# Four recurrent layers on one core: the maxima of the last attention moved among the last layer's expert pairs

## What is computed

```python
x = L0_attn_x
xn = _layernorm(x, axis=-1)
...
# layer 2: linear attention, 16 experts, 4 chosen by softmax of gates
s = _L2_attn_ref(xn, L2_attn_W_qkv, L2_attn_W_out, L2_attn_b_out)
g = _silu(_L2_ffn_ref(xn, L2_ffn_gate_w, ...))
x = x + s * g
# layer 3: softmax attention with 16 heads of 8, 64 experts, 8 chosen in groups
q, k, v = ...                                  # 16 heads, 512 x 8 each, per batch
weights = softmax(einsum('bhtk,bhsk->bhts', q, k) * scale)
out = einsum('bhts,bhsk->bhtk', weights, v)
norms = jnp.linalg.norm(out, axis=-1)
denom = jnp.maximum(norms.mean(axis=(0, 2)), 1e-05)    # over all batches
proj = (einsum('bhtk,hkd->bhtd', out / denom, Wo) + bo) * gate
s = proj.sum(axis=1) / H
g = _silu(y + shared)       # y: 64 experts of width 64, each silu(x Wg) * (x Wu) * gate, times Wd
x = x + s * g
```

## Time and profile before

| | |
|---|---|
| median of 3 runs | 3910.12 us (3902.26 to 3915.28) |
| the profiled execution | 3902.76 us |
| its span in the trace | 3901.0 us |
| PE busy | 3082.5 us, 79% of the span |
| DVE, ACT, POOL busy | 62%, 43%, 15% |
| granted TensorE clock, mean | 0.877 of full |
| HBM | 302.74 MB read, 49.66 MB written |

### The profile page before, as it was taken

How to read it: one execution, slowest core, us unless ns; L and a number is a source line. 1 busy time by engine, 2 the same in 40 slices (tenths; PEclk the granted TensorE clock), 3 DMA queues, 4 the chain that set the end, 5 groups by cost and what they waited for, 6 DMA issues and landing times.

```text
span 3901.0 us, 43769 instructions
## 1 busy us (share of the span) xinstructions
PE 3082.5 (79%) x16082; PEld 1568.3 (40%) x16174; DVE 2433.6 (62%) x4576; ACT 1661.2 (43%) x2458; POOL 598.0 (15%) x425
## 2 busy tenths in 40 slices
PE   3557868997699867998499867998689976996588
PEld 1124423553245433553245432554235532464145
DVE  4634875568656775568755776568755785533442
ACT  3404615464254624465154633456154642532231
POOL 2001101311023010321013010321013110211030
PEclk8568879998799979998799979998799988997796
DMA  3241274302842164402842046412743138412261
GB/s 111 30 90 57 47 136 122 110 23 80 134 138 67 38 100 132 138 21 62 153 128 86 20 106 116 154 33 52 133 130 101 32 84 131 134 57 62 59 198 46
DMA packets 332807, 355.92 MB, mean 91 GB/s; under 512 B 99425, under 2 KB 265121, under 8 KB 330977
## 3 DMA queue, kind: packets, MB, share of 16 engines
q1 hardware_dynamic: 332593, 353.12, 38.6%
HBM read 302.74 MB, written 49.66 MB: 90 GB/s over the span
## 4 chain that ended last, share of the span: by engine, by line
PE 52%; DVE 22%; DMA 7%; ACT 6%; issue 4%; SPq 4%; POOL 3%; another core or an unknown queue 2%; ACTq 0%; DVEq 0%; POOLq 0%
PE PS L1799 6%; PE PS L1822 5%; PE PS L1826 5%; PE PS L1653 5%; PE PS L1661 5%; DMA U<-band_scratch 4%; PE PS L1097 3%; DVE U L885 3%; PE PS L1767 3%; SPq L671 3%; DVE U L892 3%; PE PS L1778 3%; DVE MX L1590 2%; POOL D L1398 2%
## 5 line engine op out<-in xcount | busy, mean ns | idle before, releaser
L1398 POOL TENSOR_TENSOR D<-D,GW 128x512 f32<-128x512 f32 x320 | 436.0, 1364 | 1443.1 <-ACT D L1471 1205.4
L777 ACT ACTIVATE U<-U 128x2048 f32<-128x2048 f32 x256 | 487.9, 1909 | 180.1 <-DVE U L885 97.1
L1639 DVE SCALAR_TENSOR_TENSOR D<-D,PS 128x512 f32<-128x512 f32 x336 | 228.7, 681 | 408.4 <-ACT D L1475 287.5
L1471 ACT ACTIVATE D<-PS 128x512 f32<-128x512 f32 x336 | 200.1, 595 | 596.7 <-PE PS L1822 596.7
L1799 PEld LDWEIGHTS PS<-WST,D 128*128 128x128 f32 (+1 forms) x2688 | 353.4, 198 | 174.6 <-DVE D L1644 103.4
L1799 PE MATMUL PS<-WST,D 128*128 128x128 f32 (+1 forms) x2688 | 380.2, 286 | 30.2 <-DVE D L1644 30.0
L1826 PE MATMUL PS<-XT,WST 128*128 128x512 f32 (+1 forms) x672 | 371.9, 636 | 31.9 <-DVE D L1639 30.8
L892 DVE SCALAR_TENSOR_TENSOR U<-PP,RD,QB 128x512 f32<-128x512 f32 x512 | 361.9, 773 | 45.4 <-ACT QB L774 26.7
L1097 PE MATMUL PS<-U,resident 128*32 128x512 f32 x2048 | 305.1, 676 | 104.1 <-ACT U L777 104.1
L1822 PE MATMUL PS<-XT,WST 128*128 128x512 f32 (+1 forms) x672 | 367.0, 629 | 9.7 <-DMA WST<-in_pairs_dram 6.4
L1590 DVE TENSOR_REDUCE MX<-PS 128x2 f32<-128x1024 f32 x256 | 297.0, 1219 | 122.6 <-PE PS L1745 122.4
(11 more groups left out here) (345 smaller groups left out, 3878.3 us busy)
## 6 DMA issues: line engine op xcount, KB each, us to landing
GW<-gates_scratch SPq DMA_DIRECT2D x320, 256.0 KB, 4.4
WST<-in_pairs_dram SPq DMA_DIRECT2D x336, 192.0 KB, 2.4
U<-band_scratch SPq DMA_DIRECT2D x32, 1280.0 KB, 15.3
UU<-in_w_dram SPq DMA_DIRECT2D x64, 512.0 KB, 7.4
UU<-pad_scratch SPq DMA_DIRECT2D x8, 1792.0 KB
UU<-q_scratch SPq DMA_DIRECT2D x24, 384.0 KB
UU<-k_scratch SPq DMA_DIRECT2D x24, 384.0 KB
e_scratch<-D SPq DMA_DIRECT2D x8, 1024.0 KB, 4.7
```

The costliest lines, as they stand in the source:

```text
L777: e.activation(ring(i), ring(i), ACT.Gelu).then_inc(S["act"], 1)
L1398: e.tensor_tensor(AV[:, n % 3, :], AV[:, n % 3, :], GW[:, p // 2 % GWS, p % 2, :], ALU.mult).then_inc(S["gated"], 1)
```

## The change

- A third thread C (`c_pe`, `c_dve`, `c_act`, `c_sp`) takes layer 3's split, stacks, S1, maxima and their transposition. S1 uses one bank, `PZ(2)`: 64 products, each of which waits for the maximum of the one before, and 64 maxima of one bank.
- The 33 pairs of layer 3 come first, as soon as the gates are there, with C's steps among them. S2, the values and the sums' selection follow behind the pairs. The two products that spread the sums over rows are steps of S2 (the two `None` in `B_STEPS`), ACT copies them to `RC`, now in the gates' tiles (`G4`), and reciprocals read them there.
- The sum of norms (`norm_sum`, `norm_copy`, `norm_store`) is made within FFN1 of the next batch, for the last batch at the end.
- W1's first four experts are loaded into `GW` when the last gates are used, the other four into `UU` when S2 is done. FFN1 waits for the last exponential, its first `down` into `PZ(3)` for the norms.
- In layer 2 the gates' scores come ahead of q, k, v, and the gates ahead of the attention's last product. The gates' rows go through `XN` rather than `LO`.
- The loads for the end come behind the pairs of the last batch.
- All due times are new; B's steps begin earlier against A's.

```diff
-TURN = 426.70
+TURN = 425.50
...
-        w1slot = lambda x: UU[:, 2 * FF * ((x + 4) % 8):2 * FF * ((x + 4) % 8) + 2 * FF].rearrange("p (k f) -> p k f", k=2)
+        w1slot = lambda x: (GWF, UU)[x // 4][:, 2 * FF * (x % 4):2 * FF * (x % 4) + 2 * FF].rearrange("p (k f) -> p k f", k=2)
...
+            e.wait_ge(S["gate_act"], at("gate_act", b, 4))
+            e.dma_start(gw_dram, LO(b)[0:E3, :, :].rearrange("p j c -> p (j c)")).then_inc(S["gw_out"], 16)
+            yield
+            e.wait_ge(S["gw_out"], at("gw_out", b, 32))
+            for q in range(GWS):
+                gate_load(e, b, 3, q)
+            for p in range(PAIRS3):
+                yield
+                if PAIRS2 + WS + p < PAIRS:
+                    pair_load(e, b, PAIRS2 + WS + p)
+                if p % 2 == 1 and GWS + p // 2 < E3 // 4:
+                    yield
+                    gate_load(e, b, 3, GWS + p // 2)
...
+        B_STEPS = list(range(0, 42)) + [None] + list(range(42, 64)) + [None]
...
-            for k in range(32):
-                yield
-                hd, j = k // 2, 2 * (k % 2)
+        def c_dve(e, b):
...
+            for k in range(64):
+                yield
                 e.wait_ge(S["s1_3"], at("s1_3", b, k + 1))
-                e.tensor_reduce(MX3[:, j:j + 2, hd], PSall[:, 4 + j:6 + j, :], AX.X, ALU.max).then_inc(S["max3"], 1)
+                e.tensor_reduce(MX3[:, k % NT:k % NT + 1, k // NT], PSall[:, 6:7, :], AX.X, ALU.max).then_inc(S["max3"], 1)
...
+        def c_pe(e, b):
+            for k in range(64):
+                yield
+                hd, j = k // NT, k % NT
+                if k == 0:
+                    e.wait_ge(S["stacked3"], at("stacked3", b, 96))
+                    e.wait_ge(S["padded3"], at("padded3", b, 16))
+                    e.wait_ge(S["qk3"], at("qk3", b, 2))
+                else:
+                    e.wait_ge(S["max3"], at("max3", b, k))
+                e.matmul(PZ(2), QS3[:, hd, P * j:P * j + P], KS3[:, hd, :], start=True, stop=True).then_inc(S["s1_3"], 1)
...
-            weave(thread(a_pe, e, 0), thread(b_pe, e, 1))
+            weave(thread(a_pe, e, 0), thread(b_pe, e, 1), thread(c_pe, e, 1))
```

More of the change, by code:

```diff
@@ L1429, in b_act @@
             e.wait_ge(S["b_f"], at("b_f", b, 2))
+            e.wait_ge(S["gw_out"], at("gw_out", b, 16))
             e.activation(XN(b), GB(b), ACT.Tanh).then_inc(S["b_t"], 1)
-            yield from b_norm_act(e, b, 3, 151)
+            yield from b_norm_act(e, b, 3, 141)
+            yield
+            e.wait_ge(S["gate_ps"], at("gate_ps", b, 3))
+            e.activation(SCO[:, :, :], PZ(0)[:, 0:NT * E3].rearrange("p (j n) -> p j n", j=NT), ACT.Tanh, scale=0.5).then_inc(S["gate_act"], 1)
             for k in range(2):
@@ L1695, in b_pe @@
             w2 = cn("qkv2")
+            for j in range(NT):
+                last = e.matmul(PZ(0)[:, 2 * P + E2 * j:2 * P + E2 * j + E2], XT(b)[:, P * j:P * j + P], cn("gates")[:, 8:8 + E2], start=(j == 0), stop=False, skip_group_check=True)
+            last.then_inc(S["gate_ps"], 1)
             e.matmul(PZ(1), w2[:, 0:C], XT(b), start=True, stop=True).then_inc(S["l2_ps"], 1)
@@ L1699, in b_pe @@
             last.then_inc(S["l2_ps"], 1)
-            for j in range(NT):
-                e.matmul(PZ(0)[:, 2 * P + E2 * j:2 * P + E2 * j + E2], XT(b)[:, P * j:P * j + P], cn("gates")[:, 8:8 + E2], start=(j == 0), stop=False, skip_group_check=True)
             yield
+            e.wait_ge(S["gate_dve"], at("gate_dve", b, 1))
             e.wait_ge(S["l2_dve"], at("l2_dve", b, 1))
@@ L1711, in b_pe @@
             yield
+            e.wait_ge(S["gate_dve"], at("gate_dve", b, 3))
+            for j in range(NT):
+                last = e.transpose(PZ(0)[0:E2, P * j:P * j + P], GT[:, j, 0:E2], ident)
+            last.then_inc(S["gate_ps"], 1)
+            yield
             e.wait_ge(S["l2_dve"], at("l2_dve", b, 4))
@@ L1715, in b_pe @@
             last.then_inc(S["l2_ps"], 1)
-            yield
-            e.wait_ge(S["gate_dve"], at("gate_dve", b, 3))
-            for j in range(NT):
-                last = e.transpose(PZ(2)[0:E2, P * j:P * j + P], GT[:, j, 0:E2], ident)
-            last.then_inc(S["gate_ps"], 1)
             yield from b_pe_pairs(e, b, 2)
@@ L1725, in b_pe @@
             w3 = cn("wqkv3")
+            for j in range(NT):
+                last = e.matmul(PZ(0)[:, E3 * j:E3 * j + E3], XT(b)[:, P * j:P * j + P], cn("gates")[:, 24:88], start=(j == 0), stop=(j == NT - 1), skip_group_check=True)
+            last.then_inc(S["gate_ps"], 1)
             for k in range(2):
@@ L1752, in b_pe @@
             last.then_inc(S["gate_ps"], 1)
-            yield
-            e.wait_ge(S["nm3"], at("nm3", b, 1))
-            for j in range(NT):
-                last = e.transpose(PZB(1)[0:48, P * j:P * j + P], NM3[:, j, :], identb[:, :])
-            last.then_inc(S["nm_t3"], 1)
+            yield from b_pe_pairs(e, b, 3)
             def weighted(s):
@@ L1785, in b_pe, with norm_sum @@
             yield
-            e.wait_ge(S["os3"], at("os3", b, 2))
-            e.matmul(PZ(2), cn("sel_den"), OS3[:, 0, :], start=True, stop=True).then_inc(S["den3"], 1)
-            yield from b_pe_pairs(e, b, 3)
+            if b == B - 1:
+                norm_sum(e, b)
+        def norm_sum(e, b):
+            e.wait_ge(S["nrm3"], at("nrm3", b, 4))
+            for h in range(2):
+                last = e.matmul(PZ(3)[32 * h:32 * h + 8, :], cn("sum_group"), RC[:, h, :], start=True, stop=True)
+            last.then_inc(S["den3"], 1)
+        def c_pe(e, b):
+            for k in range(64):
+                yield
+                hd, j = k // NT, k % NT
+                if k == 0:
+                    e.wait_ge(S["stacked3"], at("stacked3", b, 96))
+                    e.wait_ge(S["padded3"], at("padded3", b, 16))
+                    e.wait_ge(S["qk3"], at("qk3", b, 2))
+                else:
+                    e.wait_ge(S["max3"], at("max3", b, k))
+                e.matmul(PZ(2), QS3[:, hd, P * j:P * j + P], KS3[:, hd, :], start=True, stop=True).then_inc(S["s1_3"], 1)
+            yield
+            e.wait_ge(S["nm3"], at("nm3", b, 1))
+            for j in range(NT):
+                last = e.transpose(PZB(2)[0:48, P * j:P * j + P], NM3[:, j, :], identb[:, :])
+            last.then_inc(S["nm_t3"], 1)
         def b_pe_pairs(e, b, l):
@@ L1795, in down @@
                 e.wait_ge(S["av"], at("av", b, n + 1))
-                if l == 2 and p == 0:
-                    e.wait_ge(S["l2_dve"], at("l2_dve", b, 5))
+                if p == 0:
+                    if l == 2:
+                        e.wait_ge(S["l2_dve"], at("l2_dve", b, 5))
+                    else:
+                        e.wait_ge(S["v3"], at("v3", b, 1))
                 for j in range(NT):
@@ L1854, in sp_before_final @@
                 e.wait_ge(S[s], at(s, B - 1, 0))
-            for k in range(B - 1):
+            for k in range(B - 2):
                 final_load(e, k, "fin_in")
```

319 lines of the change are left out of this document (167 added, 152 removed), and 180 rows, old and new, of tables (PER, STARTS).

## The result

| | before | with the change |
|---|---|---|
| median | 3906.68 us (4 runs) | 3976.77 us (4 runs, 3963.84 to 3980.57) |
| ratio, 95% interval | | 1.0171 (1.0140 to 1.0202) |
| span of the profiled execution | 3901.0 us | 3977.6 us |
| one full turn (mean of the seven, from one point of FFN1 to the same point) | 446.7 us | 460.2 us |

The change costs 1.7%. The forecast was 3876 us and faster; the range, up to 3940, doesn't hold it. A second measurement (e15) gave 1.0176.

A forecast was written before the change was run, and what follows sets the result against it. PE was taken as the bound: 370.8 us busy of a 447.4 us turn, plus 76.6 waiting. Seven turns +14, start -15.5, last turn -33 make -34.5 on 3901.0, so 3866.5, or 3876 on the median's scale; range 3800 to 3940.

The forecast's parts named there:

- The start, -15.5: Before the first full turn: FFN1 of batch 0 begins near 333.1 instead of 348.60, -15.5 us, bounds 0 and -15.5.
- Gates' chain, 14: Full turn after layer 3's v: PE idles 14 us while DVE makes the gates and they are spread over rows.
- Stacks, `e` and skew, 13: Full turn: gates' transfers queue behind stacks, `e` and its skewed load on SP, costing PE 13 us more idle time.
- the first product on POOL, 4: Full turn, among layer 3's pairs: the first product on POOL and its sums cost PE 4 us of idle time.
- Weights behind the bands, 11.5 + 10: Full turn: PE waits 11.5 us for pair weights behind the bands' stores, bounds 0 and 18, and 10 for bands' loads.
- The first rival: Full turn: pair weights starve behind bands' stores, PE waiting some 20 us; turn +10.5, 3935 us, slower; chance 0.23.
- The sum of the turn: Full turn: idle 52.5 us against 45.6, +7, less 5 for layer 2, rest unchanged: +2, giving 449.4.
- layer 2's -5: Layer 2: with gates first, 5 of 8.3 us of PE's waits at the gates' products and first `down` go.
- The last turn, -33: Last turn, B alone: 198 us against 225.7, -28, and layer 2's 5, together -33; bounds -20 and -42.
- No wait for L1664 above a microsecond: Sign to check in the last turn: among the pairs, no wait for L1664 should exceed a microsecond.
- the weights starve: Full turn: bands' stores hold up pair weights on SP's queue; decides from +6.9 a turn; chance 0.23.
- items 2 and 4: Full turn's idle list: gates behind stacks, `e` and skewed load (13 us); weights behind bands' stores and loads (11.5 + 10).

The follow-up runs named there:

- e15: The changed kernel again, nothing altered, run on the same chip as several follow-ups: 3980.84 us, 1.0176 to the kernel before.
- e1: The changed kernel with the bands' stores cut to 2 of 16 heads from the second batch on: 3885.62 us, 0.9937 to the kernel before.
- e3: The changed kernel with layer 3's weights from pair 5 on issued by ACT instead of SP: 3998.37 us, 1.0229 to the kernel before.
- e12: The changed kernel with FFN1 products that need nothing of A put first, and the sum of norms right at FFN1's start: 3938.51 us, 1.0067.
- e14: e12 with the bands' stores also cut to 2 of 16 heads as in e1: 3843.11 us, 0.9819 to the kernel before.
- e6: The changed kernel with bands' stores 3 and 4 behind weights of pairs 5 to 8, weights of pairs 9 to 12 among stores and bands' loads: 3973.84 us, 1.0163.
- e5: The changed kernel with bands' stores 3 and 4 moved on SP behind the weights of pairs 5 to 8: 3989.60 us, 1.0199.
- e7: The changed kernel with A's L932 ahead of B's gates on DVE and the store of `e` ahead of the stacks' loads on SP: 3984.37 us, 1.0186.
- e9: The changed kernel with the stacks' loads behind `e`'s store, skewed load and first gates on SP, and S1 later: 4147.17 us, 1.0531.
- e2: The kernel before with its bands' stores cut to 2 of 16 heads from the second batch on: 3894.30 us, 0.9960.
- e4: The changed kernel with all steps of threads B and C due 10 us later against A's: 4308.50 us, 1.1017.

## Why the prediction was wrong

**The start, -15.5: half right, on a misread row.** It came to -8.4. I took the row at 348.60 for FFN1's first product; it is the first of its second expert. The first stood at 341.81:

```profile
341.81 1.88 PE L1653 MATMUL PS<-XT,UU 128*128 128x512 f32 x4
```

With the change it stands at 317.90, ahead of the end of A. But behind the four products up of the first expert PE waits for A's reciprocal and for `mix`, so that FFN1 goes on at 340.17, not near 333.

**Gates' chain, 14: right.** 13.58.

**Stacks, `e` and skew, 13, and the first product on POOL, 4: right in kind, both too dear.** 7.2 at L1150 and 1.1 at the first product down, 8.3 together; `e` landed in 12.6.

**Weights behind the bands, 11.5 + 10: right in kind, the size near.** The weights behind L684 landed in 11.6 us. PE waits 12.7 for the pair behind the stores, and 0.8 later, 13.5; 10 for the bands' loads was too much. e1 shows that 13.9 us a turn go with the stores. The first rival, which wanted 20 there, had the sign and not the size; its 20 us of waiting were never reached. As for queue order, in e3 the weights land no sooner on another ring, so SP's order alone is not the cause.

**The sum of the turn: wrong, and this is the step that failed.** My idle time "from v to the point where A's bands are used up" was 52.5 for 45.6. From v's end to the end of A's projection it is 44.4 (122.62 less 78.18):

```profile
1905.90:2028.52 122.62, 78.18 (x415) 44.26 (x415) 74.91 (x178) 26.23 (x44) 21.55 (x17) 0.82 0.92 178
```

That is less than I said, and no more than before: 8 us too dear, which by luck hides part of the rest. The failure lies outside of it: I gave the rest of the turn nothing ("the rest of the turn keeps its work"), and that was false. Pairs, which wait for nothing of A, had stood beside A's last chain; I moved them away with the change and did not ask what they had covered. At FFN1's start PE now waits 5.2 + 4.7 + 4.0 for 3.2, 10.7 more. And it waits 6.9 for 1.0 at L1118 (L1105 before), where A's layer 0 ends: 16.6 us together.

A second part of the error is layer 2's -5, a saving of the last turn that I carried into the full turns. There was nothing to save there: in a full turn of before PE doesn't wait at L1719 and waits 2.1 at the first product down, and with the change it waits 1.2, 1.5 and 2.0 at L1771, L1780 and L1877.

Less waiting in A's layer 0 gives back 6 (3.6 for 9.7). So the sum should have read -1 for the stretch, +16.6, -6 and nothing for layer 2: some +9 or +10, with 13.5 measured. The remaining 3 to 4 I can't place; in the trace of before the missing records show as idle time, and smaller waits of the norms and of layer 2 go both ways.

What was tested of this is FFN1's start: 3938.51 us (e12) for 3980.84 (e15) on one chip, 42 of the 69 that the change costs there. The 5.9 at L1118 is read from the waits, and no run fills it. The stores and this hole are separate costs: taking both away (e14) gives 0.9819. That is a kernel with band stores left out, so it shows what the holes cost and not what can be had.

**The clock: not in the sum.** I took durations at whatever clock the rows had. Where two traces of the same PE work are complete, they differ by 24 us of PE's busy time: 3073.1 at a clock of 0.881 in e1, 3097.1 at 0.868 with the change. In e6 both kinds of turns stand in one kernel, 7 us apart. What of the change's own loss the clock makes the traces don't show.

**The last turn, -33: one term mis-sized.** The first product down came 39.8 us behind layer 3's first product (41 forecast; the gates' scores now stand there, 1.8 us ahead of q and k); S2 took 45.5 (46); the tail 13.7 (14); layer 2 gave 5.1 (5). But the 33 pairs with S1 among them took 116.4 us, from 3725.49 to 3841.9, where I took 97 with bounds of 92 and 110. PE's row in that turn, and a window of the pairs, which shows PE as the bound:

```profile
3706.21 1.03 PE L1799 MATMUL PS<-consts,G 128*64 128x128 f32 x4 [14.41 <-DVE G L1629]
...
3717.41 0.39 PE L1858 MATMUL PS<-UU 128*128 128x512 bf16 x1 [4.07 <-DMA UU<-k_scratch]
```

```profile
3730.00:3845.00 115.00, 102.66 (x447) 57.29 (x445) 80.47 (x127) 35.71 (x67) 38.29 (x30) 0.99 0.47 145
```

Gates and stacks hold the first pair as forecast. The pairs' time was there to be counted: a pair and two products of S1 take 3.14 us in the trace (1974.27 to 1977.41), 33 of them 103.6, and PE waited 10.2 for maxima on top. I had let S1's 64 products vanish into pairs that were already at PE's limit. From layer 3's first product to the norms' load it took 216.3 us for 225.7: of the 28 us that I gave to this stretch, 9.4 came. FFN1's last run took 5.6 more (53.1 for 47.4, from the first product up of its second expert to the last product up), with the norms of the batch before in it. "No wait for L1664 above a microsecond" held among the pairs but for one of 1.15; there were seventeen of them.

The rivals: "the weights starve" had the right side at 0.23, and the point from which it decides (+6.9 a turn) was passed at 13.5; but not by its mechanism alone. e1 takes 13.9 a turn away, and FFN1's start, which the rival doesn't name, costs 6 a turn beside it (42 us over seven, e12). The range ended at +10 a turn, a bound made from the transfers alone. Its lower bound of -8 doesn't follow from the list: without items 2 and 4 the 52.5 are 18, which is 28 less than 45.6. And the factor 1.0019 leaves out the 1.8 us between span and execution; 3876 is 3866.5 and the whole 9.2.

## What to carry to other kernels

When dense work is moved to cover a hole, price the place that it leaves with the same care as the place that it goes to: list who ran beside it there, and whose chain is bare afterwards. In a stretch in which the DMA engines are full, reordering the change's transfers only chose who waits (e3, e5, e6, e7, e9); taking the bands' stores out paid (e1, 13.9 us a turn). An order is worth another trial once another hole is filled: that of e6 gained nothing clear on the change and 0.0057 on e12. An engine that is busy without a gap has no room for "hidden" products: count them at full price.

## What the runs showed that I had not expected

- The same four stores of 256 KB cost 2.1 us a turn where stacks and bands stand beside them (e2) and 13.9 where weights for PE do (e1).
- Moving the weights to ACT's issue (e3) left PE's wait for them as it was, 97.5 us for 92.1, and beside the bands' transfers they took 9.1 to 12.6 us to reach PE on either queue.
- One kernel runs turns of 453.5 and of 460.3 us (e6), with PE's busy time 370.6 and 377.3 and a granted clock of 0.91 and 0.89. The order of e6 gave 0.0008 to 0.0013 on the change and 0.0057 on e12, where the clock of the turns shown is 0.91 and 0.92 with it.
- An offset of 10 us between two interleaved threads costs 332 us (e4): the due times of this kernel are made for one offset.
